# Attention scores kept in DRAM: their stores issued by ACT behind its own copies, not by SP

## Chip, core and metric

One core of one Trainium2 chip runs the whole kernel in one launch. The metric is the device time in microseconds; the times before are 1681.03, 1684.41 and 1686.25, median 1684.41.

## What is computed

3327 nodes with 256 features go through two layers. Each layer is a graph step and a mixture of 8 experts (2 chosen for each node), each on the normalised features and added to them. The change lies in the graph step of the first layer, which is an attention over all nodes:

```python
h = x @ edge_w
e = h @ h.T
e = jnp.where(adj > 0, e, NEG_BIG)
edge_att = jax.nn.softmax(e, axis=1)
combined_att = node_att * edge_att
support = x @ weight
output = adj * combined_att @ support
```

The scores e = h h^T are symmetric before the mask.

## The kernel before

`attend` works through T = 26 tiles of 128 nodes (the last is padded), every loop unrolled. For tile t the scores against all 3328 nodes are made in NC = 7 chunks of 512 columns (the last has 256), in the order `ORDER[t]`: first the chunk c = t // 4 that holds the tile's own nodes, then the later ones, then the earlier ones. "Place k" below is a chunk's place in this order. A chunk at or behind the diagonal costs TensorE six products (L941). A chunk before it (c < t // 4) is turned: its scores were already made for the other tile, so TensorE transposes four kept blocks of 128 x 128 (L936) instead. For that the chunks with c > t // 4 are kept, 84 in all (60 of 256 KB and 24 of 128 KB). Tiles 0 to 3 keep six chunks each (places 1 to 6), tiles 4 to 7 five, 8 to 11 four, 12 to 15 three, 16 to 19 two, 20 to 23 one.

A kept chunk goes this way. ACT copies it from its PSUM bank into one of KEEP_SLOTS = 3 buffers `scores_kept` (L795) and raises `raw_kept`. SP waits for `raw_kept` and stores the buffer to the tensor `raw_scores` in DRAM (L670), which raises `raw_out` of this buffer when it has landed. ACT's third copy after that waits for it. VectorE adds the mask to the scores of the same bank and takes their maximum (L856), after ACT's copy. SP later loads the chunk for another tile (L681, one of TURN_SLOTS = 6 buffers).

Each engine has its own program. ACT, step t: store the bf16 mask of tile t (L807, a DMA on ACT's queue), the exponential of tile t's scores (L809), the kept copies of tile t + 1 at places 0 to 4, the casts of tile t's transposed probabilities for groups 0 and 1 (L819), the kept copies at places 5 and 6, and then the casts of groups 2 to 6. VectorE, step t: the scores of tile t + 1 (places 0 to 4), the differences (L839) of groups 0 and 1, places 5 and 6, then groups 2 to 6; each L839 needs the cast L819 of its group. TensorE, step t: scores of tile t + 1 at places 0 to 4, the transposes (L950) of groups 0 and 1 of tile t, places 5 and 6, and then the products with the support (L976), group by group, each of which needs L839 of its group.

SP, step t, in this order: the adjacency tile t + 1 into the only buffer `adj_tile` (L704; from tile 3 on it waits for GpSimd to have read the one before), the result of tile t - 2 (L662), the normalised rows of tile t - 3 (L261), the input rows of tile t (L715), the kept stores of tile t (L670), and the turned loads for tile t + 1 (L681). GpSimd makes the mask from the adjacency tile (L767). After the stage stands a barrier of all engines.

Of the kernel before, what the change touches and what calls it, by code (L numbers as in the profile page):

```python
# [16 lines left out]
P = 128  # L17
# [10 lines left out]
CHUNKS = [(c, min(CH, NP - c)) for c in range(0, NP, CH)]  # L28
# [30 lines left out]
def unrolled(count, step):  # L59

    for t in range(count):
        step(t, t // 2, t % 2, t < 2, t == count - 1)
# [6 lines left out]
KEPT = [(t, c) for t in range(T) for c in ORDER[t] if c > t // 4]  # L69
TURNED = [(t, c) for t in range(T) for c in ORDER[t] if c < t // 4]  # L70
KEEP_SLOTS, TURN_SLOTS = 3, 6


def score_count(t, c):

    return t * NC + ORDER[t].index(c) + 1
# [523 lines left out]
def attend(nc, a, bank, gate_w, gate_b, r):  # L600

    HT, SUP, NL = a["HT"], a["SUP"], a["NL"]
    with ExitStack() as ctx:
# [10 lines left out]
        KEEP = s.sb("scores_kept", [P, KEEP_SLOTS, CH])  # L614
# [13 lines left out]
        raw_kept = s.sem("scores_copied")  # L628
        raw_out = [s.sem(f"scores_stored{i}") for i in range(KEEP_SLOTS)]
# [16 lines left out]
        def rows(dram, t):  # L646
            return dram[bass.ds(t * P, P), :]
# [3 lines left out]
        def half(slot, g):  # L651

            return (slot + g) % 2

        with nc.Block(no_gpsimd_drain=True) as block:
            @block.sync
            def _(sp):
                sp.dma_start(BB[:], a["bias"].partition_broadcast(P)).then_inc(bias_in, 16)

                def store(t, slot):  # L660
                    sp.wait_ge(out_ready, t + 1)
                    sp.dma_start(rows(a["x1"], t), XO[:, slot, :]).then_inc(x_out[slot], 16)  # L662

                def keep_scores(t):

                    for n, (row, c) in enumerate(KEPT):
                        if row == t:
                            c0, cn = CHUNKS[c]
                            sp.wait_ge(raw_kept, n + 1)
                            sp.dma_start(a["raw"][4 * c:4 * c + cn // P, t // 4, :, t % 4, :].rearrange("r p n -> p r n"),  # L670
                                         KEEP[:, n % KEEP_SLOTS, 0:cn].rearrange("p (r n) -> p r n", n=P)).then_inc(raw_out[n % KEEP_SLOTS], 16)

                def load_scores(m):

                    t, c = TURNED[m]
                    kept = KEPT.index((4 * c + 3, t // 4)) + 1
                    for i in range(KEEP_SLOTS):
                        sp.wait_ge(raw_out[i], (kept + KEEP_SLOTS - 1 - i) // KEEP_SLOTS * 16)
                    if m >= TURN_SLOTS:
                        sp.wait_ge(qk_done, score_count(*TURNED[m - TURN_SLOTS]))  # L680
                    sp.dma_start(TURN[m % TURN_SLOTS], a["raw"][t, c].rearrange("p j n -> p (j n)")).then_inc(raw_in[m % TURN_SLOTS], 16)  # L681

                loads = [0]

                def load_scores_until(t):

                    upto = min(len(TURNED), sum(row <= t for row, c in TURNED) + TURN_SLOTS)
                    upto = min(upto, sum(row <= t + 1 for row, c in TURNED))
                    for m in range(loads[0], upto):
                        load_scores(m)  # L690
                    loads[0] = max(loads[0], upto)

                def step(t, uses, slot, first, last):
                    base = (T - 1) * P
                    tail = ((0, TAIL_A), (TAIL_A, TAIL))
                    nxt = t + 1
                    if 2 <= nxt < T:
                        if nxt > 2:
                            sp.wait_ge(mask_ready, nxt - 2)
                        if nxt == T - 1:  # L700
                            for lo, hi in tail:
                                sp.dma_start(ADJ[lo:hi, 0:N], a["adj"][base + lo:base + hi, :]).then_inc(adj_in, 16)
                        else:
                            sp.dma_start(ADJ[:, 0:N], rows(a["adj"], nxt)).then_inc(adj_in, 16)  # L704
                    if not first:
                        store(t - 2, slot)
                    if t >= 3:
                        gate.store(sp, t - 3, 1 - slot)
                    if t >= 2:
                        sp.wait_ge(x_ready, t - 1)  # L710
                    if last:
                        for lo, hi in tail:
                            sp.dma_start(XB[lo:hi, slot, :], a["x"][base + lo:base + hi, :]).then_inc(x_in[slot], 16)
                    else:
                        sp.dma_start(XB[:, slot, :], rows(a["x"], t)).then_inc(x_in[slot], 16)  # L715
                    keep_scores(t)
                    load_scores_until(t)
                unrolled(T, step)
                gate.store(sp, T - 3, (T - 3) % 2)
                for t in (T - 2, T - 1):  # L720
                    store(t, t % 2)
                    gate.store(sp, t, t % 2)
                gate.end(sp)
                for slot in range(2):
                    sp.wait_ge(x_out[slot], T // 2 * 16)
                for i in range(KEEP_SLOTS):
                    sp.wait_ge(raw_out[i], (len(KEPT) + KEEP_SLOTS - 1 - i) // KEEP_SLOTS * 16)
# [54 lines left out]
            @block.scalar  # L782
            def _(act):
                gate.load(act)

                def keep_scores(t, places):

                    for k in places:
                        c = ORDER[t][k]
                        if (t, c) in KEPT:  # L790
                            n, cn = KEPT.index((t, c)), CHUNKS[c][1]
                            act.wait_ge(qk_done, score_count(t, c))
                            if n >= KEEP_SLOTS:
                                act.wait_ge(raw_out[n % KEEP_SLOTS], n // KEEP_SLOTS * 16)
                            act.copy(KEEP[:, n % KEEP_SLOTS, 0:cn], bank[k % 4][:, 0:cn]).then_inc(raw_kept, 1)  # L795

                def step(t, uses, slot, first, last):
                    if first and slot == 0:
                        act.wait_ge(nmx_ready, 1)
                        act.activation(NATT[:], NL[:], ACT.Exp, bias=NSM[:, 1:2], accum_out=NSM[:, 2:3]).then_inc(e_ready, 1)  # L800
                    if last:
                        act.wait_ge(qk_done, T * NC)
                        act.dma_start(a["FIRST"][:], a["w_in"][0][:, :, 0:2 * H0]).then_inc(first_in, 16)
                        act.dma_start(a["FIRST_OUT"][:], a["w_out"][0][:, :, 0:D]).then_inc(first_in, 16)
                    if not first:
                        act.wait_ge(mask_ready, t - 1)
                    act.dma_start(a["mask"][t, :, :], NEG[:, slot, :]).then_inc(mask_out[slot], 16)  # L807
                    act.wait_ge(neg_max, t + 1)
                    act.activation(SC[:, slot, :], SC[:, slot, :], ACT.Exp, bias=SM[:, slot, 0:1],  # L809
                                   accum_out=SM[:, slot, 1:2]).then_inc(exp_done, 1)  # L810
                    if not last:
                        keep_scores(t + 1, range(NC - 2))
                    for g, (g0, gn) in enumerate(GROUPS):
                        if g == EARLY and not last:
                            keep_scores(t + 1, range(NC - 2, NC))
                        act.wait_ge(flipped, t * NG + g + 1)
                        if not (first and slot == 0 and g < 2):
                            act.wait_ge(pv_group, t * NG + (g - 1))
                        act.copy(PT[:, half(slot, g), 0, 0:gn * P], bank[4 + half(slot, g)][:, 0:gn * P]).then_inc(hi_ready, 1)  # L819
                        if t >= 1 and g == 2:  # L820
                            gate.copy_rows(act, t - 1, 1 - slot)
                        if t >= 1 and g == 4:
                            gate.exp(act, t - 1, 1 - slot)
                keep_scores(0, range(NC))
                unrolled(T, step)
                gate.copy_rows(act, T - 1, (T - 1) % 2)
                gate.exp(act, T - 1, (T - 1) % 2)
                act.wait_ge(first_in, 32)
                for slot in range(2):
                    act.wait_ge(mask_out[slot], T // 2 * 16)  # L830
# [958 lines left out]
```

## Time and profile before

| | |
|---|---|
| profiled execution, device time | 1686.91 us |
| its span | 1685.2 us |
| runs | 1681.03, 1684.41, 1686.25 us |
| mean granted TensorE clock | 0.953 |
| busy share of the span: TensorE, VectorE, GpSimd, ACT | 88%, 59%, 49%, 39% |
| attention stage | from 87.4 us to about 630 us |

The profile is one execution; times in it are from the span's start. A line of the timeline gives start, duration, engine, source line, operation, tensors, and how often it stands there in a row; in brackets the idle time of the engine before it and what ended this. SPq and ACTq lines are issues of DMAs on the queues of SyncE (SP) and ScalarE (ACT).

### The profile page before, as it was taken

The numbers are of one execution on the slowest core, as the hardware profiler recorded it, in microseconds if no ns is written. First come the engines' busy times: TensorE is split into PE (matmuls) and PEld (weight loads), VectorE is DVE, ScalarE is ACT, GpSimd is POOL, SyncE is SP. The second block draws the span as 40 slices with busy tenths as digits, with TensorE's granted clock in tenths as the row PEclk, the third lists the DMA queues.
The fourth block names the chain that finished last, engine by engine and source line by source line (L and its number), as shares of the span: only waits on it lengthen the run. The fifth ranks groups of instructions, "written<-read, shape, count | busy, mean of one in ns | idle before, by whom it ended". The sixth has DMA issues, their size and how long they took to land. (4 is left out here: it accounts for less than half of the span.)

```text
span 1685.2 us, 36741 instructions
## 1 busy us (share of the span) xinstructions
PE 1478.3 (88%) x9748; PEld 1275.2 (76%) x9748; DVE 998.1 (59%) x3423; ACT 664.7 (39%) x1485; POOL 825.4 (49%) x1603
## 2 busy tenths in 40 slices
PE   5789999999999957989999827999749999999994
PEld 5779999999999956777778703555438889888894
DVE  5535666666667744555555363677656655666652
ACT  2434444444444322222222241111125565555563
POOL 0013444445545535666666502788744545555552
PEclk9989999999999978999999958999969999999997
DMA  4156666667777524653333369798535632222223
GB/s 134 62 188 205 210 213 215 229 221 234 238 249 244 177 71 123 146 122 48 49 50 50 44 158 186 152 177 163 99 91 151 165 71 39 36 37 37 37 38 100
DMA packets 247537, 221.66 MB, mean 132 GB/s; under 512 B 120363, under 2 KB 226729, under 8 KB 243929
## 3 DMA queue, kind: packets, MB, share of 16 engines
q1 hardware_dynamic: 213784, 161.71, 35.0%
q0 software_dynamic: 25984, 31.06, 11.4%
q10 hardware_dynamic: 7680, 27.84, 4.6%
q8 instruction: 38, 0.62, 0.2%
q14 instruction: 51, 0.42, 0.1%
HBM read 127.29 MB, written 74.52 MB: 120 GB/s over the span
## 5 line engine op out<-in xcount | busy, mean ns | idle before, releaser
L1182 PE MATMUL bank<-ffn_w_in_parts,ffn_x_t 128*128 128x512 f32 x1416 | 362.1, 403 | 17.8 <-DVE ffn_x_t L1298 14.3
L1182 PEld LDWEIGHTS bank<-ffn_w_in_parts,ffn_x_t 128*128 128x128 f32 x1416 | 258.8, 190 | 77.1 <-DVE ffn_x_t L1298 17.6
L1206 PE MATMUL bank<-ffn_w_out_parts,ffn_hidden_t 128*128 128x256 f32 x2124 | 283.5, 287 | 16.7 <-DVE ffn_hidden_t L1305 16.6
L976 PE MATMUL bank<-support,attn_probs_t 128*128 128x256 f32 x2028 | 284.9, 291 | 11.8 <-DVE attn_probs_t L839 11.5
L1206 PEld LDWEIGHTS bank<-ffn_w_out_parts,ffn_hidden_t 128*128 128x128 f32 x2124 | 261.6, 191 | 22.3 <-issue 17.0
L976 PEld LDWEIGHTS bank<-support,attn_probs_t 128*128 128x128 f32 x2028 | 256.5, 192 | 16.8 <-issue 12.3
L1146 POOL DMA_INDIRECT x<-ffn_y,ffn_dst x118 | 196.1, 1662 | 53.2 <-issue 51.1
L1501 PE MATMUL bank<-normed_parts,nbr_adj_t 128*128 128x512 f16 x676 | 164.7, 390 | 39.9 <-DVE nbr_adj_t L1620 35.7
L1248 ACT ACTIVATE ffn_silu_or_gelu<-bank,w_b_in 128x128 f32<-128x128 f32 x472 | 134.3, 367 | 143.7 <-PE bank L1193 143.7
L819 ACT CAST attn_probs_t<-bank 128x512 fp32r<-128x512 f32 (+1 forms) x182 | 98.7, 558 | 221.8 <-PE bank L950 221.6
L839 DVE TENSOR_TENSOR attn_probs_t<-bank,attn_probs_t 128x512 fp32r<-128x512 f32 (+1 forms) x182 | 116.2, 650 | 92.3 <-ACT attn_probs_t L819 91.9
L1305 DVE TENSOR_TENSOR ffn_hidden_t<-ffn_silu_or_gelu,ffn_hidden_t 128x512 fp32r<-128x512 f32 x118 | 81.0, 692 | 125.6 <-ACT ffn_hidden_t L1254 125.1
L1501 PEld LDWEIGHTS bank<-normed_parts,nbr_adj_t 128*128 128x128 f16 x676 | 65.8, 102 | 108.1 <-issue 44.0
L856 DVE CUSTOM_DVE_ANT_0 attn_scores<-bank,attn_mask 128x512 f32<-128x512 f32 (+1 forms) x182 | 113.3, 649 | 55.1 <-PE bank L941 43.4
L941 PE MATMUL bank<-h_t,attn_h_tile 128*128 128x512 f32 (+1 forms) x660 | 140.8, 368 | 2.9 <-POOL attn_identity L733 2.9
L941 PEld LDWEIGHTS bank<-h_t,attn_h_tile 128*128 128x128 f32 x660 | 115.3, 190 | 23.2 <-POOL attn_identity L733 3.1
L1135 POOL DMA_INDIRECT ffn_x_gathered<-xn,ffn_tok x118 | 122.2, 1036 | 17.2 <-issue 1.1
L245 POOL TENSOR_TENSOR attn_rstd<-attn_mean_var,attn_constants 128x1 f32<-128x1 f32 x26 | 4.8, 186 | 233.7 <-DVE attn_mean_var L231 233.7
L950 PE MATMUL bank<-attn_identity,attn_scores 128*128 128x128 f32 x676 | 101.9, 277 | 3.1 <-ACT attn_scores L809 3.1
L1193 PE MATMUL bank<-ffn_identity,ffn_hidden 128*128 128x128 f32 x708 | 97.0, 273 | 2.9 <-DVE ffn_hidden L1293 2.1
L1145 POOL TENSOR_TENSOR ffn_wait_taker<-ffn_identity 128x1 f32<-128x1 f32 x118 | 24.7, 210 | 150.0 <-DVE ffn_y L1356 118.7
L1131 POOL COPY ffn_tok<-ffn_pairs 128x1 int32 (+1 forms) x118 | 86.8, 736 | 5.8 <-PE bank L1171 3.7
(273 smaller groups left out, 2342.2 us busy)
## 6 DMA issues: line engine op xcount, KB each, us to landing
adj_tile<-in_adj SPq DMA_DIRECT2D x25, 1663.5 KB, 8.0
mask<-attn_mask ACTq DMA_DIRECT2D x26, 832.0 KB, 3.5
raw_scores<-attn_scores_kept SPq DMA_DIRECT2D x60, 256.0 KB, 2.3
first_w_in<-raw_scores SPq DMA_DIRECT2D x48, 256.0 KB, 3.6
w_w_in<-in_w SPq DMA_DIRECT2D x28, 256.0 KB
w_w_in<-in_w_t SPq DMA_DIRECT2D x28, 256.0 KB
w_w_out<-in_w_t SPq DMA_DIRECT2D x28, 256.0 KB
first_w_out<-raw_scores SPq DMA_DIRECT2D x24, 256.0 KB, 3.7
```

What stands on the lines that cost most here:

```text
L819: act.copy(PT[:, half(slot, g), 0, 0:gn * P], bank[4 + half(slot, g)][:, 0:gn * P]).then_inc(hi_ready, 1)
L839: dve.tensor_tensor(PT[:, half(slot, g), 1, 0:gn * P], bank[4 + half(slot, g)][:, 0:gn * P], PT[:, half(slot, g), 0, 0:gn * P].bitcast(F32 ...
L856: dve.tensor_tensor_reduce(out=SC[:, slot, c0:c0 + cn], in0=bank[k % 4][:, 0:cn], in1=NEG[:, slot, c0:c0 + cn], scale=1.0, scalar=-3.0e38, ...
L941: ins = pe.matmul(bank[k % 4][:, 0:cn], HS[:, slot, hs, kd, :], HT[:, hm, kd, c0:c0 + cn], start=n == 0 and kd == 0, stop=n == 2 and kd == ...
L950: ins = pe.transpose(bank[4 + half(slot, g)][:, j * P:(j + 1) * P], SC[:, slot, (g0 + j) * P:(g0 + j + 1) * P], ID[:])
L976: ins = pe.matmul(bank[6 + slot][:, 0:D], part[:, hp, :], SUP[:, jt, hs, :], start=jt == 0 and n == 0, stop=jt == T - 1 and n == 2)
L1135: pool.indirect_dma_start(out=XG[:, slot, :], out_offset=None, in_=a["xn"], in_offset=bass.IndirectOffsetOnAxis(ap=TOKS[:, slot:slot + 1], ...
L1146: pool.indirect_dma_start(out=acc, out_offset=bass.IndirectOffsetOnAxis(ap=DSTS[:, slot:slot + 1], axis=0), in_=YS[:, slot, :], in_offset= ...
L1182: ins = pe.matmul(bank[2 + 2 * slot + b][:, :], XT[:, slot, xp, k, :], WIP[:, wp, k, b * CH:(b + 1) * CH], start=n == 0 and k == 0, stop=n ...
L1206: ins = pe.matmul(bank[7][:, 0:D], HTT[:, hp, k, :], WOP[:, wp, k, :], start=n == 0 and k == 0, stop=n == 2 and k == KH - 1)
L1248: ins = act.activation(GATE[:, j, k * P:(k + 1) * P], src[:, k * P:(k + 1) * P], ACT.Gelu, bias=w.BI[:, bass.ds(e * KH + (4 * j + k), 1)])
L1501: ins = pe.matmul(bank[2 + slot][:, :], AT[:, slot, g0 + j, :], XH[:, g0 + j, :, :].rearrange("p a d -> p (a d)"), start=g0 + j == 0, stop ...
```

## The change

SP no longer stores the kept chunks. ACT does, right behind each copy: it waits for its own copy's semaphore, and then issues the same DMA from the same buffer to the same place, with the same semaphore raised. Nothing else is changed: the waits of SP's turned loads and of ACT's copies on `raw_out` stay as they are.

```diff
-                def keep_scores(t):
-
-                    for n, (row, c) in enumerate(KEPT):
-                        if row == t:
-                            c0, cn = CHUNKS[c]
-                            sp.wait_ge(raw_kept, n + 1)
-                            sp.dma_start(a["raw"][4 * c:4 * c + cn // P, t // 4, :, t % 4, :].rearrange("r p n -> p r n"),
-                                         KEEP[:, n % KEEP_SLOTS, 0:cn].rearrange("p (r n) -> p r n", n=P)).then_inc(raw_out[n % KEEP_SLOTS], 16)
-
...
                         sp.dma_start(XB[:, slot, :], rows(a["x"], t)).then_inc(x_in[slot], 16)
-                    keep_scores(t)
                     load_scores_until(t)
...
                             act.copy(KEEP[:, n % KEEP_SLOTS, 0:cn], bank[k % 4][:, 0:cn]).then_inc(raw_kept, 1)
+                            act.wait_ge(raw_kept, n + 1)
+                            act.dma_start(a["raw"][4 * c:4 * c + cn // P, t // 4, :, t % 4, :].rearrange("r p n -> p r n"),
+                                          KEEP[:, n % KEEP_SLOTS, 0:cn].rearrange("p (r n) -> p r n", n=P)).then_inc(raw_out[n % KEEP_SLOTS], 16)
```

## Rows read from the trace of the kernel before

**Rows 1.** The page: busy time by engine, and one kind of DMA issue.

```profile
PE 1478.3 (88%) x9748; PEld 1275.2 (76%) x9748; DVE 998.1 (59%) x3423; ACT 664.7 (39%) x1485; POOL 825.4 (49%) x1603
...
mask<-attn_mask ACTq DMA_DIRECT2D x26, 832.0 KB, 3.5
```

**Rows 2.** Busy time in the stretch with tile 3's scores, clock behind POOL.

```profile
149.30:171.20 21.90, 21.90 (x156) 20.32 (x155) 13.04 (x56) 10.56 (x18) 9.47 (x17) 1.00 0.72 213
```

**Rows 3.** ACT's timeline: tile 0's last copies, tile 1, tile 3, a mask store.

```profile
98.02 1.09 ACT L795 COPY attn_scores_kept<-bank 128x512 f32<-128x512 f32 x2 [0.77 <-PE bank L941]
99.13 1.28 ACT L800 ACT_TABLE_LOAD   x1
...
103.80 1.53 ACT L795 COPY attn_scores_kept<-bank 128x512 f32<-128x512 f32 x3
110.84 0.59 ACT L795 COPY attn_scores_kept<-bank 128x512 f32<-128x512 f32 x1 [5.52 <-DMA raw_scores<-attn_scores_kept]
...
156.28 0.59 ACT L795 COPY attn_scores_kept<-bank 128x512 f32<-128x512 f32 x1 [1.48 <-DMA raw_scores<-attn_scores_kept]
...
168.49 0.34 ACTq L807 DMA_DIRECT2D mask<-attn_mask  x1
168.88 3.08 ACT L809 ACTIVATE attn_scores<-attn_scores,attn_small 128x3328 f32<-128x3328 f32 x1
```

**Rows 4.** SyncE's timeline: adjacency tile 2 and tile 1's stores.

```profile
99.59 0.49 SPq L704 DMA_DIRECT2D adj_tile<-in_adj  x1
...
104.38 9.45 SPq L670 DMA_DIRECT2D raw_scores<-attn_scores_kept  x6
```

**Rows 5.** DMA issues from 99.5 to 104 us; last figure: us to landing.

```profile
adj_tile<-in_adj SPq DMA_DIRECT2D x1, 1663.5 KB, 8.8
mask<-attn_mask ACTq DMA_DIRECT2D x1, 832.0 KB, 9.6
```

**Rows 6.** All issues of kept stores, in ns, and their landing times.

```profile
L670 SPq DMA_DIRECT2D raw_scores<-attn_scores_kept x84: 359/372/1667, 93.2 to 545.4; - x84
...
DMA to landing us min/median/max: 1.8/2.3/6.7
```

**Rows 7.** TensorE's timeline around the gap in tile 1.

```profile
106.16 2.34 PE L941 MATMUL bank<-h_t,attn_h_tile 128*128 128x512 f32 x12
112.82 2.93 PE L976 MATMUL bank<-support,attn_probs_t 128*128 128x256 f32 x12 [4.33 <-DVE attn_probs_t L839]
...
119.08 1.68 PE L976 MATMUL bank<-support,attn_probs_t 128*128 128x256 f32 x12
...
120.95 1.68 PE L976 MATMUL bank<-support,attn_probs_t 128*128 128x256 f32 x12
```

**Rows 8.** Busy time and clock (third figure from the end) in this gap.

```profile
108.50:112.80 4.30, 0.00 (x0) 0.00 (x0) 1.33 (x5) 1.96 (x5) 1.21 (x2) 0.86 0.88 279
```

**Rows 9.** Timeline of all engines, tile 4's scores at place 4.

```profile
177.47 0.59 ACT L795 COPY attn_scores_kept<-bank 128x512 f32<-128x512 f32 x1 [0.77 <-PE bank L941]
177.95 1.08 ACT L819 CAST attn_probs_t<-bank 128x512 fp32r<-128x512 f32 x2
178.70 1.28 DVE L839 TENSOR_TENSOR attn_probs_t<-bank,attn_probs_t 128x512 fp32r<-128x512 f32 x2
...
179.53 0.71 PE L976 MATMUL bank<-support,attn_probs_t 128*128 128x256 f32 x4
```

**Rows 10.** Timeline of all engines, tile 9's scores from place 1 on.

```profile
279.12 3.63 SPq L670 DMA_DIRECT2D raw_scores<-attn_scores_kept  x4
...
281.22 1.08 ACT L795 COPY attn_scores_kept<-bank 128x512 f32<-128x512 f32 x2 [0.77 <-PE bank L941]
282.37 1.07 ACT L819 CAST attn_probs_t<-bank 128x512 fp32r<-128x512 f32 x2
...
283.83 0.83 PE L976 MATMUL bank<-support,attn_probs_t 128*128 128x256 f32 x5 [0.18 <-DVE attn_probs_t L839]
```

**Rows 11.** ACT's timeline, tile 12's casts behind its kept copies.

```profile
342.54 1.09 ACT L819 CAST attn_probs_t<-bank 128x512 fp32r<-128x512 f32 x2 [0.50 <-PE bank L950]
```

## The prediction

> **What bounds the kernel now.** I read the page first: TensorE is busy for 88% of the span [rows 1], and the next engines are far below it. The change touches only the attention stage (87 to 630 us), so I cut that stage into its tiles of 128 nodes. Tile 3's stretch (149.3 to 171.2 us) has TensorE busy for 21.90 of 21.90 us at full clock, and in tile 9 it waits for only 0.18 us before the first product with new probabilities [rows 10]. So TensorE's own stream sets the pace there: a delay of its next instruction is paid in full, and a delay of any other engine is free until TensorE waits for it. After the stage everything starts behind a barrier, so what the attention gains or loses reaches the end undiminished.
>
> Then I asked who waits for a kept store. ACT does, at two places. The larger is in the scores of tile 1: the copy at place 4 starts at 110.84, after 5.52 us of idling for a store [rows 3]. The reader should see why the store was late. SyncE sends the next adjacency tile (1,663.5 KB) only at 99.59, because in its program order the six stores of tile 0 stand ahead of it, and the last of these waits for a copy that ends at 98.02 + 1.09 = 99.11 [rows 3, 4]. The adjacency tile needs 8.8 us to land, and tile 1's stores, from 104.38 on, are on the same queue behind it: one needs 6.7 us instead of the usual 2.3 [rows 4 to 6]. TensorE pays twice. Its last product before the gap ends at 106.16 + 2.34 = 108.50, the next starts at 112.82, 4.3 us later [rows 7]. And the granted clock falls from full speed (2.4 GHz) to half (1.2 GHz): its mean over the 4.3 us is 0.86, so the last 4.3 x 0.14 / 0.5 = 1.2 us were at half, and TensorE had done nothing for 3 us when it fell [rows 8]. Therefore from 112.82 to 119.08 it does two groups of products that take 120.95 - 119.08 = 1.87 us each at full clock, so 6.26 - 3.74 = 2.5 us went to the clock [rows 7].
>
> The second wait for a store (1.5 us, in tile 3, at 156.28 [rows 3]) costs nothing, since TensorE is busy for the whole of that stretch [rows 2].
>
> **The change, part by part.** (1) SyncE loses 84 issues and 84 waits for copies. Its own time is worth nothing, but what stood behind them moves forward: the adjacency tile 2 goes out with the stage's first loads, near 88 us, instead of at 99.59, and has landed some 9 us later, before tile 1's first store leaves. Tile 0's stores, from 93 us on, share the DMA engines with it; I cost that at nothing, as a late landing there holds up a copy first and TensorE only through it. In other tiles the adjacency load waits for GpSimd's mask anyway and moves by under 3 us; GpSimd uses it a tile later.
>
> Now tile 1. Its first stores leave with only the mask store of tile 0 ahead of them (832 KB, which took 9.6 us beside the adjacency load, [rows 5], and by then is nearly done). So I take the usual landing, 2.3 us [rows 6].
>
> (2) ACT gains, behind each copy, a wait for the copy's own end and an issue. An issue on ACT's queue takes 0.34 us, and what follows starts 168.88 - 168.83 = 0.05 later [rows 3]; the same store on SyncE takes 0.36 to 0.37 [rows 6]. SyncE's issue at 104.38 comes as the copy from 103.80 ends (0.59 later) [rows 3, 4], so the wait adds nothing else. That makes 0.42 us. Also, without the wait ACT starts its next operation 0.48 us after the start of a copy that lasts 0.59 [rows 9], and this overlap goes. From copy to next operation: 0.59 + 0.42 = 1.01 instead of 0.48, for a copy of 256 columns 0.37 + 0.42 = 0.79. Copies at places 1 to 3 come every 1.36 us, as the scores do (0.59 and 0.77 of idling for TensorE [rows 9]), so there 1.01 is hidden.
>
> (3) At the last copy before TensorE's turn to the transposed probabilities it isn't hidden: behind it on ACT stand the two casts at L819, for these VectorE's differences (L839), and for these TensorE (L976).
> - Tiles 4 to 7: copy at 177.47, first cast at 177.95, and at 1.01 it starts at 178.48, ends at 179.07. The difference started at 178.70 (VectorE had been busy), now at 179.10: +0.4. TensorE follows at 179.53 + 0.4 [rows 9]. Four times 0.4 = 1.6.
> - Tiles 8 to 11: two copies, the second of 256 columns, stand there. 281.22 + 1.01 + 0.79 = 283.02 against 282.37: +0.65; TensorE had waited for this very chain already (0.18) [rows 10]. Four times 0.65 = 2.6.
> - Tiles 12 to 15: the same pair, but then ACT idled for 0.50 before its cast [rows 11]. The pair takes 1.80 instead of 1.08 [rows 10], so 0.72 - 0.50 = 0.2. Four times 0.2 = 0.8.
> - Tiles 16 to 23: one or two copies, with three or more turned chunks between them and the cast. Nothing.
> - Tiles 2 and 3: tile 3 took its 1.5 us stall without loss [rows 2, 3], so they have 1.5 us of cover. 0 to 0.2 in all.
> Loss: 1.6 + 2.6 + 0.8 = 5.0, with tile 3 up to 5.2.
>
> (4) The gain in tile 1. The last two copies of tile 0 take 1.80 instead of 1.09, and ACT's table load behind them moves from 99.13 to 99.8, so the first copy of tile 1 goes from 103.80 to 104.5 [rows 3]. Place 4 comes three steps of 1.01 later, at 107.5; its buffer is free when the store issued at 105.1 has landed, 107.4. So 107.6 instead of 110.84. The cast comes 1.01 behind it instead of 0.48, so the whole chain to TensorE is 2.7 us earlier: TensorE starts at 110.1, not 112.82, and idles 1.6 us instead of 4.3. The clock stayed full through the first 3 us of idling before [rows 8], so I take it as kept: 2.5 us more. Gain: 2.7 + 2.5 = 5.2.
>
> Sum: -5.2 + 5.0 to 5.2 = about 0. SyncE's loads of turned scores also leave earlier, by some 4 us (in tile 9 from behind the stores, which end at 279.12 + 3.63, to ahead of 279.12 [rows 10]), among the stores. For that I add 0.5. The profiled execution took 1686.9 us (span 1685.2), the median of three is 1684.4, 2.5 us less; on the median it is 1684.4 + 0.5, rounded to 1685.0.
>
> On this last point the Trainium skill speaks against the change ("DMA: Bandwidth & Descriptors", section "Issuing engines are not separate DMA queues"): DMAs of different engines share the 16 DMA engines and interleave, and another issuer saves only the issue time. The trace agrees so far as it shows it: the mask store from ACT's queue took 9.6 us beside the adjacency load, against a median of 3.5 [rows 1, 5]. By the rule alone there would be no gain at all; the gain that I count comes from the order of the transfers, which the rule doesn't cover.
>
> **Rivals.**
> *A, slower: the turned loads collide with the stores.* Place: tiles 8 to 11, where place 4 needs the buffer of place 1. The store of place 1 leaves at 279.12, the copy at place 4 starts at 281.22 + 1.01 = 282.23 [rows 10]: it waits as soon as a landing takes over 3.1 us, against 2.3 now. Two loads of 256 KB in front would take 2 x 0.9 us (832 KB take about 3 us of the 3.5 us that a mask store mostly needs [rows 1]), so landing at 4.1 and 1.0 us a tile; tile 7, with two loads, 0.7; tile 11, with three, 0.9 more. 4.0 + 0.7 + 0.9 = 5.6: 1690. For it: loads and stores now never overlap here. Against: the loads would leave before the store and be half through.
> *B: tile 1's stall stays*, because the mask store or an adjacency load (of tile 3) is in the way again. Then only the 5.2 of loss is left: 1690. Against: that load can't leave before GpSimd has made mask 2, some 3 us after the mask store, and by then the store that matters is under way.
> *C: the issue is cheaper on ACT* than on SyncE, as it overlaps with the copy's end. With half the 0.53, the loss is 2 and the gain 5.9: 1680.5. Against: the wait comes before the issue in program order.
> *D: the clock falls after 1.6 us too.* Then +3.0: 1687.5.
>
> **How the numbers follow.** Forecast 0.58, A 0.13, B 0.10, C 0.10, D 0.05, others 0.04. The issue's cost is bounded below by 0 (C and more) and above by the longest issue of this store, 1.7 us, once in 84 [rows 6]. What can be told from no change is 0.3%, or 5.1 us: under 1679.4 or over 1689.5. Two thirds of A and B lie above, and a little of the others: slower 0.16. C lies just inside: faster 0.06. Same 0.78. The range that leaves out 2 in 10 runs from 1680 to 1690.5.
>
> **What would show it.** In the changed profile: the adjacency load of tile 2 near 88 us; ACT's wait for stores in tile 1 near 0 and TensorE's gap near 1.6 us at full clock; store issues on ACT's queue of 0.36 us; the cast of tiles 4 to 7 1.0 us after the last copy; TensorE's wait for L839 at each tile's first product longer by 0.4 (tiles 4 to 7), 0.65 (8 to 11) and 0.2 us (12 to 15). The prediction is wrong if ACT waits for stores in tiles 4 to 11, if stores from ACT's queue take over 3.1 us to land, or if the gap in tile 1 is still over 3 us.

## The result, and the profile after

The changed kernel took 1688.38 us (median of 20 runs, 1681.69 to 1693.08), the kernel before 1682.53 (20 runs, 1675.43 to 1689.48): ratio 1.003, 95% interval 1.0018 to 1.0043, some 3 to 7 us slower. The time lies in the predicted range, and 0.3% is the bound that the prediction drew between no change and slower. But the interval excludes no change, while the sum of the prediction came out at about nothing.

Single runs scatter by more than that. So does the part behind the attention stage, which the change doesn't touch: from the last result of the stage to the end of the span it took between 1064.3 and 1074.7 us in the nine profiles of this document. In the two profiles compared here it was 4.9 us shorter after than before, which hides the loss of the stage in these two (spans 1685.7 and 1685.2 us). Within the attention stage the trace is steady: the results of two tiles that nothing touches leave SyncE 17.84 us apart in every profile. So I took, from SyncE's timeline, the issue of each tile's result (L662). The time between two of them is one period; it holds the scores of one tile (the one named below) and the products of the tile before. The first runs from TensorE's first score product to the first result; it holds tile 0 and tile 1's scores.

```
period, by the         before   after against
scores in it             us     before, us       predicted
0 and 1                39.37      -2.99            -5.2
2, 3                   21.8        0.0, 0.0        0 to 0.2 in all
4, 5, 6, 7             21.2       +0.81 +0.46 +0.48 +0.48    +0.4 each
8, 9, 10, 11           20.4       +1.06 +1.42 +0.80 +0.79    +0.65 each
12, 13, 14, 15         19.5       +0.36 each                 +0.2 each
16, 17, 18, 19         18.6       +0.26 +0.23 +0.24 +0.26    0
20 to 25               17.6        0.0             0
tile 25's products     20.29      -0.75            not foreseen
whole stage           527.86      +4.94            0, and +0.5 for the loads
```

The two queues, from the instructions and waits of `scores_kept` in the changed kernel (issue times in ns; then idle time of ACT, in us and times, by what ended it; then landings in us):

```profile
L788 ACTq DMA_DIRECT2D raw_scores<-attn_scores_kept x84: 365/366/412, 93.7 to 551.7; - x84
...
  DMA raw_scores<-attn_scores_kept: 6.7, 7
...
DMA to landing us min/median/max: 1.9/3.2/9.8
```

The issue by itself takes what was predicted. But the profile now names a store seven times as what ACT waited for, not twice, and the median landing went from 2.3 [rows 6] to 3.2 us. Two of the seven, 0.50 us in tile 0 and 0.49 us in tile 11, are no longer than what an issue alone puts between two copies (below); the other five lie in tiles 0, 3, 4, 8 and 9.

ACT's timeline, tiles 0 and 1 (beside [rows 3]):

```profile
98.06 0.59 ACT L786 COPY attn_scores_kept<-bank 128x512 f32<-128x512 f32 x1 [1.68 <-DMA raw_scores<-attn_scores_kept]
...
99.15 0.59 ACT L786 COPY attn_scores_kept<-bank 128x512 f32<-128x512 f32 x1 [0.50 <-DMA raw_scores<-attn_scores_kept]
...
101.03 1.28 ACT L794 ACT_TABLE_LOAD   x1 [0.43 <-ACT attn_scores_kept L786]
...
105.69 0.57 ACT L786 COPY attn_scores_kept<-bank 128x512 f32<-128x512 f32 x1
...
108.91 0.59 ACT L786 COPY attn_scores_kept<-bank 128x512 f32<-128x512 f32 x1 [0.49 <-PE bank L935]
...
109.94 1.07 ACT L813 CAST attn_probs_t<-bank 128x512 fp32r<-128x512 f32 x2 [0.44 <-ACT attn_scores_kept L786]
```

The 5.52 us stall before place 4 is gone: that copy comes at 108.91 straight behind the one before. But there is a new wait of 1.68 us in tile 0, and the table load is at 101.03 instead of 99.13. TensorE's timeline there (beside [rows 7]), and its clock (third figure from the end) in two stretches:

```profile
107.17 2.34 PE L935 MATMUL bank<-h_t,attn_h_tile 128*128 128x512 f32 x12
111.30 2.25 PE L970 MATMUL bank<-support,attn_probs_t 128*128 128x256 f32 x12 [1.79 <-DVE attn_probs_t L833]
...
116.60 1.68 PE L970 MATMUL bank<-support,attn_probs_t 128*128 128x256 f32 x12
```
```profile
109.50:111.30 1.80, 0.01 (x2) 0.00 (x1) 1.44 (x5) 1.36 (x3) 1.04 (x2) 1.00 0.91 262
111.30:113.30 2.00, 2.00 (x12) 2.00 (x13) 1.90 (x10) 0.57 (x2) 1.91 (x3) 0.72 0.46 134
```

The gap shrank from 4.3 to 1.79 us. Yet the clock fell to half all the same, only later: a mean of 0.72 over 2 us means 2 x 0.28 / 0.5 = 1.1 us at half, so it fell near 112.2, with TensorE at work again; it was back at full near 115.6, after 3.4 us at half. The two groups take 116.60 - 111.30 = 5.30 us instead of 3.74.

Timeline of all engines in tile 6 (periods of +0.48) and tile 9 (+1.42), beside [rows 9, 10]:

```profile
218.61 0.59 ACT L786 COPY attn_scores_kept<-bank 128x512 f32<-128x512 f32 x1 [0.78 <-PE bank L935]
219.23 0.37 ACTq L788 DMA_DIRECT2D raw_scores<-attn_scores_kept  x1
219.69 1.07 ACT L813 CAST attn_probs_t<-bank 128x512 fp32r<-128x512 f32 x2 [0.49 <-PE bank L944]
220.31 1.29 DVE L833 TENSOR_TENSOR attn_probs_t<-bank,attn_probs_t 128x512 fp32r<-128x512 f32 x2 [0.38 <-ACT attn_probs_t L813]
...
221.15 1.07 PE L970 MATMUL bank<-support,attn_probs_t 128*128 128x256 f32 x7 [0.55 <-DVE attn_probs_t L833]
```
```profile
279.91 0.40 ACTq L788 DMA_DIRECT2D raw_scores<-attn_scores_kept  x1
280.04 0.86 SPq L672 DMA_DIRECT2D first_w_in<-raw_scores  x2
...
283.71 0.37 ACT L786 COPY attn_scores_kept<-bank 128x256 f32<-128x256 f32 x1 [1.11 <-DMA raw_scores<-attn_scores_kept]
...
286.03 0.71 PE L970 MATMUL bank<-support,attn_probs_t 128*128 128x256 f32 x4 [1.60 <-DVE attn_probs_t L833]
```

In tile 6 the cast comes 1.08 us behind the copy's start: 0.59 for the copy and 0.49 until ACT goes on. The bracket puts these 0.49 down to TensorE; but the issue on ACT's queue fills 219.23 to 219.60 of it, and the issue is what held ACT. In tile 9, SyncE sends two turned loads at 280.04, 0.13 us behind the first store, and the copy that needs that store's buffer idles until 283.71, 0.62 later than the issues alone would have it (1.11 - 0.49).

### The profile page after: what moved, and what is told of

Read it like the earlier page. It is cut to its first block and busy times, and to the rows that moved or that the text cites. A ratio compares the mean times of both kernels' runs of the same rounds, so it can differ in the third digit from the quotient of the medians.

```text
span 1685.7 us, 36741 instructions
## 1 busy us (share of the span) xinstructions
PE 1477.5 (88%) x9748; PEld 1273.8 (76%) x9748; DVE 1000.1 (59%) x3423; ACT 664.9 (39%) x1485; POOL 821.4 (49%) x1603
## 5 line engine op out<-in xcount | busy, mean ns | idle before, releaser
L1129 POOL DMA_INDIRECT ffn_x_gathered<-xn,ffn_tok x118 | 122.8, 1040 | 17.2 <-issue 1.1
```

What stands on the lines that cost most here:

```text
L1129: pool.indirect_dma_start(out=XG[:, slot, :], out_offset=None, in_=a["xn"], in_offset=bass.IndirectOffsetOnAxis(ap=TOKS[:, slot:slot + 1], ...
```

## The experiments

The periods are against the kernel before, as in the table above, and each is from one profile. The kernel before was run again beside two groups of experiments: 1687.0 us (20 runs) beside the first four, 1688.73 us (11 runs) beside the last three. Four experiments have one run each, which says nothing about the whole time at this scatter; their periods are what counts.

**The issues moved behind the casts.** ACT still stores, but the last one or two stores of a tile wait on its program until its two early casts are out.

```diff
+                            pending.append((n, t, c, cn))
+                            last_two = [m for m, (row, cc) in enumerate(KEPT) if row == t and ORDER[t].index(cc) < NC - 2][-(1 if 0 < t < 8 else 2):]
+                            if t == 0:
+                                last_two = [4, 5]
+                            if n not in last_two:
+                                flush()
...
+                        if g == EARLY:
+                            flush()
```

> The changed kernel, but ACT issues the stores of the last copy (tiles 1 to 7) or the last two (tiles 8 to 23) before its two early casts only behind these casts; those of tile 0's last two copies behind the mask store. Theory 1 (the loss in tiles 4 to 19 is the issue time that ACT spends between copy and cast, 0.49 us each, reaching TensorE through the casts or through VectorE's masking): the periods of tiles 4 to 19 go back to those of the kernel before, within 0.1 us but for 0.3 to 0.6 us in two or three tiles where a store lands late, and the whole is 6 to 8 us faster than the changed kernel, some 2 to 4 us faster than the kernel before. Rival (the loss is late landings of stores that share the DMA engines with SP's loads): tiles 4 to 19 keep their 0.3 to 1.4 us each.

1686.44 us (12 runs) against 1687.0 (ratio 1.000, 0.9985 to 1.0014). The periods of tiles 5 to 7, 8 and 11 to 19 are back within 0.1 us; tiles 4, 9 and 10 keep 0.37, 0.68 and 0.66. So the loss in tiles 4 to 19 is where ACT issues, to the place, but for some 1.7 us of late landings. The whole gained less than I expected, since the first period stayed at -3.29: the three issues between tile 1's copies are still there, and in this run TensorE was at half clock up to 93 us and more, from the stage's start at 87.25, where it had been full from 91 on before; tile 0's transposes begin 18.9 us into the stage instead of 17.2. Also, one of the issues that I had moved behind the mask store took 1.06 us, and the exponential behind it came after 1.41 us of idling. The clock didn't fall in tile 1 here, after a gap of 1.47 us.

**The adjacency tile first, nothing else.** SP stores as before.

```diff
+                    if t == 0:
+                        sp.dma_start(ADJ[:, 0:N], rows(a["adj"], 2)).then_inc(adj_in, 16)
                     keep_scores(t)
                     load_scores_until(t)
```

> The kernel before (SP stores), with one thing of the change alone: the adjacency tile 2 is sent ahead of tile 0's kept stores. If the change's gain in tile 1 comes from the place of this transfer, the gap of TensorE in tile 1 shrinks from 4.3 to under 1.5 us, tile 0's stores wait behind it on the same queue (copies 4 and 5 some 1 to 3 us late), tiles 2 to 25 keep the periods of the kernel before, and the whole is 2 to 5 us faster than before. If the gain needs the stores on another queue, tile 0's stall eats it: within 1 us of before.

1679.31 us (9 runs) against 1687.0: ratio 0.996 (0.9944 to 0.9977), more than the 2 to 5 us that I expected. First period -6.51, all others within 0.1. TensorE's timeline:

```profile
106.59 2.34 PE L943 MATMUL bank<-h_t,attn_h_tile 128*128 128x512 f32 x12
108.87 1.69 PE L978 MATMUL bank<-support,attn_probs_t 128*128 128x256 f32 x12
110.40 0.60 PE L952 MATMUL bank<-attn_identity,attn_scores 128*128 128x128 f32 x4
```

No gap and full clock: all of the 4.3 + 2.5 = 6.8 us that [rows 7] showed, but for 0.3. ACT still waits for stores twice (1.5 us each, in tiles 0 and 1), and little of it reaches TensorE: its transposes begin 17.63 us into the stage, 0.4 later than in the kernel before (17.22).

**The wait alone.** `act.wait_ge(raw_kept, n + 1)` behind each copy, with SP issuing the store.

> The kernel before, with ACT waiting for its own copy's end but SP still issuing the store. It prices the wait alone. Theory 1: the wait costs the lost overlap, 0.1 to 0.15 us for a copy, so tiles 4 to 15 are 0 to 0.2 us longer each and the rest of the loss (0.25 to 0.65) belongs to the issue. Rival (the wait with its semaphore round trip is most of the price): tiles 4 to 7 get 0.4, tiles 8 to 11 0.7 us longer here too.

Tiles 4 to 15: 0.02 to 0.07 us longer each; the first period -0.01. The wait costs next to nothing, the issue costs the rest. (One run, 1692.56 us; the stage, 528.17 us, is 0.3 longer than before, so the rest of that time lies outside it.)

**Six buffers instead of three** in the changed kernel (`KEEP_SLOTS = 6`).

> The changed kernel with KEEP_SLOTS 6 instead of 3, so that no copy waits for a store. What late landings cost goes: in tile 0 (2.2 us of waits, which delay the exponential and tile 1's chain) and in tiles 4, 8 and 9 (0.3 to 0.6 us above their neighbours). Theory 1: tiles 5 to 7 keep +0.5, 10 and 11 +0.8, 12 to 15 +0.36, 16 to 19 +0.25 against before; stage 0 to 1 is 1 to 2 us shorter than in the changed kernel. Rival (landings are the whole of the loss): all tiles go back to before.

One run, 1689.39 us. ACT waits for no store. First period -5.18; tile 4 +0.48, tiles 5 to 7 +0.45 to 0.49; 8 to 11 all +0.79 or 0.80; 12 to 15 +0.36; 16 to 19 +0.24 to 0.29 with one of 0.52. This separates the two losses: late landings took 0.33 in tile 4, 0.27 in 8, 0.62 in 9, and 2.2 us in the first period. Of these 2.2, 0.7 are the waits in tile 0 (the table load comes 11.7 us into the stage, not 12.4). The rest is the clock, which stayed full here after a gap of 1.62 us. The table load is now 0.74 us later than in the kernel before on the stage's own time, which is the 0.7 of the prediction.

**The adjacency tile first, with six buffers**: SP stores, as in the second experiment. This is the fastest version found.

```diff
-KEEP_SLOTS, TURN_SLOTS = 3, 6
+KEEP_SLOTS, TURN_SLOTS = 6, 6
```

> The best version so far (SP stores, adjacency tile 2 sent ahead of tile 0's stores) with KEEP_SLOTS 6 instead of 3. It takes away the two waits for stores that are left there (1.5 us each, in tiles 0 and 1). Theory: both are under cover (TensorE has no gap in tile 1 there), so every tile keeps its period within 0.1 us, and the whole is again 5 to 8 us faster than the kernel before. Rival: these waits still cost, and the stretch to tile 0's result is 1 us or more shorter.

1677.4 us (6 runs) against 1688.73: ratio 0.9944 (0.9925 to 0.9964), so 6 to 13 us faster, where I expected 5 to 8. The first period is -7.17, 0.66 less than with three buffers, so the two waits weren't wholly covered, as I had expected, and cost less than the 1 us of the rival. Tiles 2 to 25 are within 0.1; the products of tile 25 read -1.45, by the clock (see below). The interval overlaps with that of the adjacency tile first, so that six buffers add anything isn't shown; that the place of the transfer does is.

**The other queue without the other place.** The changed kernel, with one wait on SP.

```diff
+                        if nxt == 2:
+                            sp.wait_ge(raw_kept, NC - 1)
```

> The changed kernel (ACT stores), but SP sends the adjacency tile 2 only after tile 0's six copies, as in the kernel before. It tells whether the gain in tile 1 comes from the place of this transfer or from the other queue. Theory (the place): ACT waits 2 us or more for a store in tile 1 again, and the stretch to tile 0's result is within 1.5 us of the kernel before or longer, by the issues. Rival (the queue: stores on ACT's queue need not stand behind the adjacency load): landings in tile 1 stay under 4 us and the gain of 3 us stays or grows, as tile 0's stores are then free of the load.

One run, 1698.57 us. The stall is back, on ACT's own queue. ACT's timeline, then the last store of tile 0 and the first two of tile 1 among the DMA issues (us to landing last):

```profile
109.00 0.59 ACT L788 COPY attn_scores_kept<-bank 128x512 f32<-128x512 f32 x1 [1.84 <-DMA raw_scores<-attn_scores_kept]
...
111.56 0.59 ACT L788 COPY attn_scores_kept<-bank 128x512 f32<-128x512 f32 x1 [1.97 <-DMA raw_scores<-attn_scores_kept]
```
```profile
raw_scores<-attn_scores_kept ACTq DMA_DIRECT2D x1, 128.0 KB, 8.5
...
raw_scores<-attn_scores_kept ACTq DMA_DIRECT2D x2, 256.0 KB, 5.1
```

First period +0.24. Tile 0's last store was issued at 100.39, beside the adjacency load (100.38) and ahead of the mask store (101.37); it took 8.5 us, and the copy at 109.00 waited for it. Tile 1's first two still take 5.1 us beside the adjacency load (and behind the mask store), against 6.7 behind that load on its own queue. The Trainium skill ("DMA: Bandwidth & Descriptors", section "Issuing engines are not separate DMA queues") says that DMAs issued by different engines run on the same 16 DMA engines and interleave there, and this trace agrees: 8.5 and 5.1 us on the other queue, against the usual 2.3. In tile 0, all of whose copies now come ahead of the load, no copy waits for a store. The gain was the place, not the queue. This kernel's tile 8 also shows what a wait can cost: 1.7 us for a store made a gap of 2.17 us on TensorE, the clock fell 1.1 us behind its end, and the period was 3.50 us longer (tile 9 read +1.28, the others about what the changed kernel has, or less).

**The turned loads held** until the tile's last kept copy, in the changed kernel.

```diff
+                    sp.wait_ge(raw_kept, sum(row <= t for row, c in KEPT))
                     load_scores_until(t)
```

> The changed kernel, with SP holding a tile's turned loads until its last kept copy is made, as they stood in the kernel before. Theory: what tiles 4, 8 and 9 have above their neighbours (0.33, 0.27 and 0.62 us) comes from these loads running beside the stores, so ACT's waits for stores there go and the tiles read +0.5, +0.8, +0.8 against before; tiles 12 to 19 keep +0.36 and +0.25. Rival (other traffic delays these stores): two or three tiles still have waits of 0.5 to 1.5 us for a store.

One run, 1693.42 us. Tile 4 +0.47 instead of 0.81, tile 9 +0.85 instead of 1.42: there it was the loads. Tile 8 kept +0.98 and a wait of 0.59 us for a store, so other traffic can do it too; which, stays open. The wait also stands in tile 0, ahead of the adjacency load, which I had overlooked: the first period went to +0.79 with the same two waits in tile 1 (1.85 and 1.98 us). So on the first period this run only repeats the one before it; what it has more comes from the stage's start, where TensorE was at half clock until 92.8, for 6.8 us instead of 3.4. Tiles 10 and 11 read +0.86 and +0.87, tiles 12 to 15 +0.42: some 0.06 more than without the hold.

## Why the prediction was right or wrong

**How right.** The sum was +0.5 us, and the stage became 4.9 us longer; the time still fell into the range. Part of that is luck: the forecast stood on a median of 1684.4 us for the kernel before, from three runs, and twenty runs gave 1682.53. On that base the range would have ended near 1688.6, and 1688.38 would have been just inside. Of the three signs that the prediction named against itself, two came: ACT waits for stores in tiles 4, 8 and 9, and the median landing is 3.2 us, over the 3.1 that it set. The third did not: the gap in tile 1 is 1.79 us, not over 3.

**Right:** TensorE's stream sets the pace (the periods came back, one by one, with the issues deferred). The place of the gain and its cause. The path of the loss in tiles 4 to 15, from the issue over the two casts and VectorE's difference to TensorE. Tiles 2 and 3 covered, 20 to 23 free.

**The issue was sized too small.** I took 0.42 us from the end of a copy to ACT's next operation, from the row of a mask store; it is 0.49. The last pair of copies then takes 1.08 + 0.86 = 1.94 us, not 1.80. In tiles 8 to 11 that is 1.94 - 1.15 = 0.79, where I had 0.65, and in tiles 12 to 15, where the casts used to start 1.59 behind the pair's start, 0.35, where I had 0.2. Over tiles 4 to 19 the six-buffer run has 7.5 us of issue cost (7.8 with its one odd period); I had 5.0.

**Tiles 16 to 19 were not "nothing".** I followed the casts alone. There they have room, but VectorE doesn't: it can mask the second kept chunk only after ACT's copy, and this copy now waits for the first one's issue. Timelines before, then after:

```profile
417.36 1.08 ACT L795 COPY attn_scores_kept<-bank 128x512 f32<-128x512 f32 x2 [1.34 <-PE bank L941]
...
418.61 0.42 DVE L856 CUSTOM_DVE_ANT_0 attn_scores<-bank,attn_mask 128x256 f32<-128x256 f32 x1
...
421.03 1.68 PE L976 MATMUL bank<-support,attn_probs_t 128*128 128x256 f32 x12 [0.37 <-DVE attn_probs_t L839]
```
```profile
422.60 0.58 ACT L786 COPY attn_scores_kept<-bank 128x512 f32<-128x512 f32 x1 [1.33 <-PE bank L935]
...
424.09 0.42 DVE L850 CUSTOM_DVE_ANT_0 attn_scores<-bank,attn_mask 128x256 f32<-128x256 f32 x1 [0.17 <-issue]
...
426.50 1.68 PE L970 MATMUL bank<-support,attn_probs_t 128*128 128x256 f32 x12 [0.61 <-DVE attn_probs_t L833]
```

From the first copy to the masking of the second chunk: 1.25 us before, 1.49 after. TensorE's wait grows by the same 0.24. This path costs 1.0 us in the four tiles.

**The gain in tile 1** was 3.0 instead of 5.2. The step that failed is "I cost that at nothing" for tile 0's stores beside the adjacency load: they landed late (the wait of 1.68 us; with the load held back there was none), and with the issues the table load came 1.4 us later on the stage's own time (101.03 - 99.13, less the 0.5 by which the stage began later), not 0.7. So TensorE started 2.0 us earlier, not 2.7, and the gap was 1.79 us, not 1.6. The second is the clock: a fall after the shorter gap was rival D, at 0.05. It cost 5.30 - 3.74 = 1.6 of the 2.5 us; 2.0 + 0.9 is the measured 3.0. The gaps of 1.47 and 1.62 us in two experiments kept full clock, so this was decided by little. It is read from one profile (a run of 1687.51 us); in how many of the 20 runs the clock fell there isn't known.

**Rival A** came true in part: the loads collide in tiles 4 and 9, for 0.3 and 0.6 us, not in every tile from 7 on; late landings took 1.2 us in tiles 4 to 11, against its 5.6 and the 0.5 in the sum. **B** didn't come, nor did **C**: nothing of the issue is hidden under the copy.

Altogether, 2.2 us of gain were missing, and the loss was 8.7 instead of 5.0 (1.2 of it landings). Tile 25's products, 0.75 us shorter, gave some back. Both kernels have the same gap there, of 3.1 us. TensorE's timelines, before, then after:

```profile
598.21 1.09 PE L950 MATMUL bank<-attn_identity,attn_scores 128*128 128x128 f32 x8 [3.12 <-ACT attn_scores L809]
```
```profile
604.41 1.97 PE L944 MATMUL bank<-attn_identity,attn_scores 128*128 128x128 f32 x8 [3.11 <-ACT attn_scores L803]
```

Before, the eight transposes behind the gap run at full clock, and it falls 1.5 us after the gap's end; after, it fell 0.7 us before that end. In both it is at half for 6.8 us, and after the change more of these lie in the idle time. In the experiments this term is between -0.09 and -1.45 us, with the same gap. That is not the change's doing in any way that I could show.

## What to carry to other kernels

An issue of 0.37 us on an engine that computes is paid wherever its next operation is on the way to the bound engine; follow all that it delays, also what another engine does later in its own order. When a wait goes away with an issuer, ask which transfer moved, and make that move alone: here one line (the big load ahead of the small stores) gave 4 to 9 us, while the change of issuer that contained the same move lost 3 to 7. Issue a store where the engine would idle anyway, and not between the last copy and the cast that the product waits for.

## What I hadn't expected of the hardware

After a gap of 1.79 us TensorE's clock was still full and fell 0.9 us later, with the engine at work; after 1.62 and 1.47 us it stayed full, and after 2.17 us it fell, 1.1 us into the work. A gap can so be paid for after its end: here at half speed (1.2 GHz) for 3.4 us. The length of the gap doesn't settle when: two gaps of 3.1 us, one in each kernel, had the fall 1.5 us after the end and 0.7 us before it. And ACT goes on only 0.09 us after its queue has issued a kept store (219.60 to 219.69 in tile 6), where a mask store had shown 0.05.
